# Fused joins, gate logits from joined rows, and scatters spread over three steps in a four-layer transformer kernel

## The chip, the core and the metric

The kernel runs on one core of a Trainium2 chip. The metric is the device time of one execution in microseconds (us). Matrix products run on TensorE (PE in the profile; its weight loads are PEld), element-wise work on VectorE (DVE), ScalarE (ACT) and GpSimd (POOL), and SyncE (SP) issues most of the transfers. The engines run in parallel, each takes its own instructions in program order, and they wait for each other by semaphores. Indirect transfers (scatters and gathers by index) are issued by GpSimd.

## What is computed

Two transformer layers on x of shape 4 x 512 x 256, each of an attention part and a feed-forward part. Every part takes normalised rows and is joined by another normalisation:

```python
x = x + _layernorm(_L0_attn_ref(_layernorm(x), ...))   # rms norm, rope, 16 heads, causal, + bo + residual
x = x + _layernorm(_L0_ffn_ref(_layernorm(x), ...))    # 8 experts, top 2, capacity 640 rows each
x = x + _layernorm(_L1_attn_ref(_layernorm(x), ...))   # causal attention
x = x + _layernorm(_L1_ffn_ref(_layernorm(x), ...))    # 8 small experts and a shared one, dense
```

The residual inside the first attention is its own input, the normalised rows. The first feed-forward sends rows to experts:

```python
probs = jax.nn.softmax(xr @ Wg, axis=-1)
gate_vals, expert_idx = jax.lax.top_k(probs, K)
pos = jnp.sum((jnp.cumsum(oh, axis=0) - 1) * oh, axis=1)      # rank of a row in its expert
kept = pos < C
dispatched = xr[dispatch_mask.reshape(-1) % S].reshape(E, C, d)
```

## The kernel before

The 2048 rows of x lie in SBUF as 16 tiles of 128 rows (`x`), with a second buffer of the same size (`sub`) for normalised rows and for the outputs of a part. The program is a chain of phases with a barrier of all engines between two: set-up, attention 0, experts, attention 1, dense.

**An attention phase** (`attention_phase`) walks 16 steps T, four head groups (g = T mod 4) for each of four batches (b = T div 4), and two steps behind them for what lags. A step has eleven slots s. In slot s TensorE fills a score bank whose row maxima VectorE takes (`unit_max`), and a second bank, three slots behind, that ScalarE turns into exponentials. GpSimd zeroes the upper triangle of these (`causal`, L494) at slots 0, 2 and 7. P·V of step T-2 stands at slots 2 and 5 of step T and waits for the selects. All other matrix work shares two banks in turn (`ps_m`): transposes, projections, P·V transposes ("otr"), output transposes ("ot"), output projections ("out"), and for the routing "rt" (transposes of the rows), "lg" (gate logits) and "rk" (ranks). `misc_plan` writes by hand in which step and slot each is filled and emptied. A filling waits until the last but one on its bank is empty. All engines walk the same slots in order, so one late engine holds the others back.

**Layer 0's extras.** GpSimd makes the residual (L513 and L516: normalised rows plus output bias), and VectorE adds it to the output projection's result (L1111), takes statistics, gets 1/sigma from GpSimd (`root`, a power), normalises `sub` tile by tile (L1135), adds it to x (L1141), and takes the new statistics. Only with the new mean and 1/sigma do `route_rows` (L1153) make normalised rows, which are transposed, multiplied by the gate weights, and go through `choose_top`, `choose_at`, `count`, `place` to a slot in the experts' buffer. `scatter` (L554) sends each tile by two indirect transfers. Batch 0's tiles are scattered in step 14, batch 1's in step 17, batches 2 and 3 behind the loop. The first expert's weights w1 are loaded at step 11, and split into a high and a low part in one piece each at step 13 (ScalarE L809, GpSimd L624).

**The passage to the experts.** The phase ends when all scatters have landed. After the barrier, `expert_phase` loads the first expert's rows (L1652), transposes them, and starts its matmuls.

**Attention 1** first gathers the experts' outputs (L562), weights and joins them (`combine_sum`, `combine_normalise`, `combine_add`), two batches ahead of its loop and two in it. **The dense phase** is one stream of matmuls; its last batch is joined behind the last of them by the class `Joining`.

## Time and profile before

| | us |
|---|---|
| median of 3 runs | 1114.74 |
| lowest and highest | 1113.88, 1115.35 |
| the profiled execution | 1114.21 |
| its span, first to last instruction | 1111.8 |

| engine | busy us | share of the span |
|---|---|---|
| TensorE | 943.1 | 85% |
| VectorE | 611.4 | 55% |
| ScalarE | 473.8 | 43% |
| GpSimd | 455.5 | 41% |

A busy share is an average over stages with different limits. The page's slices show TensorE below half of its time around 300 to 345 us (the passage to the experts) and again near 580 to 605 us (the passage to attention 1). Its clock is granted at two levels, full (1.00 in the rows) and half (0.50); a value between is an average over a stretch. Matmuls are pipelined, so that the durations of successive ones overlap: what one more costs is the distance of two starts. A row of a timeline gives start, duration, engine, line, operation, output and inputs, the count of merged instructions, and in brackets how long the engine had idled and for whom.

### The profile page before, as it was taken

How to read it: one execution, taken by the hardware profiler on the slowest of the kernel's cores; microseconds unless marked ns; L12 is line 12 of the kernel's file. 1: busy time of each engine (PE TensorE's matmuls, PEld its weight loads, DVE VectorE, ACT ScalarE, POOL GpSimd, SP SyncE). 2: the span in 40 equal slices, each digit the busy share in tenths (PEclk: the TensorE clock that was granted, in tenths of full speed). 3: DMA queues.
4: the chain of work that ended last, by engine and by line, in shares of the span. 5: the costliest groups of instructions: out<-in, count | busy, mean ns of one | idle time of the engine just before them, and what ended most of it. 6: DMA issues, size and time to landing. Idle time of an engine off the chain costs nothing. (4 is left out here: it accounts for less than half of the span.)

```text
span 1111.8 us, 17858 instructions
## 1 busy us (share of the span) xinstructions
PE 943.1 (85%) x6122; PEld 760.3 (68%) x6122; DVE 611.4 (55%) x1970; ACT 473.8 (43%) x838; POOL 455.5 (41%) x429
## 2 busy tenths in 40 slices
PE   3799999868418999999982779899999779999996
PEld 1467767645318999999981446566667558888885
DVE  7577787956613343333435766776666334553534
ACT  2156555634103343333336245556556433343331
POOL 3354653555441333222336523445243534634232
PEclk9799999978757999999995889999999979999998
DMA  4443213210123323333103752532410010000001
GB/s 138 170 158 101 86 30 124 68 52 1 48 73 141 116 99 117 123 123 123 61 27 110 219 183 81 164 98 91 161 59 29 1 48 1 1 20 1 20 1 38
DMA packets 50312, 91.78 MB, mean 83 GB/s; under 512 B 7360, under 2 KB 23104, under 8 KB 50112
## 3 DMA queue, kind: packets, MB, share of 16 engines
q1 hardware_dynamic: 47168, 82.49, 22.3%
q0 software_dynamic: 3072, 8.39, 2.4%
q8 instruction: 38, 0.62, 0.2%
q14 instruction: 34, 0.28, 0.1%
HBM read 54.55 MB, written 36.31 MB: 82 GB/s over the span
## 5 line engine op out<-in xcount | busy, mean ns | idle before, releaser
L795 ACT ACTIVATE a_probs<-a_ps_b 128x512 f32<-128x512 f32 x320 | 187.4, 602 | 171.1 <-PE a_ps_b L859 168.7
L1063 DVE CUSTOM_DVE_ANT_0 a_masked_s<-a_ps_a,a_mask_f 128x512 f32<-128x512 f32 (+1 forms) x256 | 154.4, 621 | 116.0 <-PE a_ps_a L843 110.7
L843 PE MATMUL a_ps_a<-a_k_st,a_q_st 128*128 128x256 f32 (+3 forms) x512 | 191.3, 421 | 15.7 <-DMA a_k_st<-scratch 12.5
L494 POOL TENSOR_SCALAR_AFFINE_SELECT a_probs<-a_probs 128x512 f32<-128x512 f32 x128 | 79.6, 639 | 182.7 <-ACT a_probs L795 182.3
L1711 POOL TENSOR_TENSOR w_lo<-w_raw,w_hi 128x2048 fp32r<-128x2048 f32 x16 | 74.0, 4627 | 174.1 <-ACT w_hi L1728 174.1
L859 PE MATMUL a_ps_b<-a_q_less,a_k_st 128*128 128x384 f32 (+3 forms) x512 | 133.0, 323 | 6.6 <-ACT a_probs L795 5.5
L843 PEld LDWEIGHTS a_ps_a<-a_k_st,a_q_st 128*128 128x128 f32 x512 | 96.0, 199 | 55.7 <-issue 34.2
L859 PEld LDWEIGHTS a_ps_b<-a_q_less,a_k_st 128*128 128x128 f32 x512 | 89.2, 191 | 30.1 <-ACT a_probs L795 22.0
L883 PE MATMUL a_ps_pv<-a_probs,a_v 128*32 128x512 f32 (+3 forms) x1024 | 90.4, 476 | 8.8 <-POOL a_probs L494 8.8
L1926 POOL TENSOR_TENSOR dense_h_lo<-dense_mixed,dense_h_hi 128x512 fp32r<-128x512 f32 x40 | 52.2, 1306 | 102.5 <-ACT dense_h_hi L1983 102.5
L1776 DVE SCALAR_TENSOR_TENSOR exp_h_lo<-exp_ps_u,exp_h_hi 128x320 fp32r<-128x320 f32 x128 | 61.4, 490 | 59.0 <-ACT exp_h_hi L1737 58.2
L1822 PE MATMUL exp_ps_o<-w_hi,exp_h_hi 128*128 128x256 f32 x320 | 92.5, 289 | 0.0
L1737 ACT ACTIVATE exp_h_hi<-exp_ps_u 128x320 fp32r<-128x320 f32 x128 | 54.2, 438 | 89.6 <-PE exp_ps_u L1804 89.6
L1822 PE MATMUL exp_ps_o<-w_hi,exp_h_lo 128*128 128x256 f32 x320 | 90.4, 283 | 0.0
L1822 PE MATMUL exp_ps_o<-w_lo,exp_h_hi 128*128 128x256 f32 x320 | 90.4, 283 | 0.0
L1804 PE MATMUL exp_ps_u<-exp_x_t_hi,w_hi 128*128 128x320 f32 x256 | 80.4, 314 | 1.1 <-DVE exp_x_t_lo L1756 1.1
L1804 PE MATMUL exp_ps_u<-exp_x_t_lo,w_hi 128*128 128x320 f32 x256 | 80.2, 313 | 0.0
L1804 PE MATMUL exp_ps_u<-exp_x_t_hi,w_lo 128*128 128x320 f32 x256 | 80.2, 313 | 0.0
L883 PEld LDWEIGHTS a_ps_pv<-a_probs,a_v 128*32 128x32 f32 x1024 | 28.2, 116 | 66.7 <-issue 55.2
L2164 DVE TENSOR_TENSOR dense_product<-dense_gated,dense_ps_u 128x512 f32<-128x512 f32 x40 | 27.5, 687 | 78.5 <-PE dense_ps_u L2000 72.8
L1822 PEld LDWEIGHTS exp_ps_o<-w_lo,exp_h_hi 128*128 128x128 f32 x320 | 61.3, 191 | 0.0
L1822 PEld LDWEIGHTS exp_ps_o<-w_hi,exp_h_lo 128*128 128x128 f32 x320 | 61.3, 191 | 0.0
(267 smaller groups left out, 2217.6 us busy)
## 6 DMA issues: line engine op xcount, KB each, us to landing
w_raw<-in_m_w SPq DMA_DIRECT2D x16, 1024.0 KB, 5.7
scratch<-a_hi SPq DMA_DIRECT2D x24, 512.0 KB, 2.8
scratch<-a_lo SPq DMA_DIRECT2D x24, 256.0 KB, 3.4
a_q_st<-scratch SPq DMA_DIRECT2D x64, 96.0 KB, 2.6
a_k_st<-scratch SPq DMA_DIRECT2D x64, 96.0 KB, 2.6
exp_rows<-dispatched SPq DMA_DIRECT2D x9, 640.0 KB, 3.9
dispatched<-kept_sub SPq DMA_DIRECT2D x9, 512.0 KB, 2.9
results<-exp_out SPq DMA_DIRECT2D x7, 640.0 KB, 4.0
```

Of the source, the lines that this page charges most:

```text
L494: nc.gpsimd.affine_select(out=blocks, in_=blocks, compare_op=ALU.is_ge, fill=0.0, base=0, pattern=[[0, HPG], [1, P]], channel_multiplier=- ...
L795: nc.scalar.activation(probs[:, k, :], ps_b[k % B_BANKS][:, :], ACT.Exp, scale=scale).then_inc(exps, 1)
L843: last = nc.tensor.matmul(ps[:, at:at + wd], q_st[t % STACKS][:, h // PER_TILE, i * P:wd], k_st[t % STACKS][:, h, 0:wd], start=True, stop= ...
L859: last = nc.tensor.matmul(ps[:, at:at + wd], k_st[t % STACKS][:, h, j * P:(j + 1) * P], q_less[:, h // PER_TILE, j * P:SEQ], start=True, s ...
L883: last = nc.tensor.matmul(ps_pv[h * VW:(h + 1) * VW, at:SEQ], v[:, b % 2, j, g * HPG + h, :], rhs, start=(j == 0), stop=(j == 2), skip_gro ...
L1063: nc.vector.tensor_tensor_reduce(masked_s[n % 2][:, 0:wd], ps[:, 0:wd], mask_f[:, SEQ - wd:SEQ], -1.0, -NEG, ALU.add, ALU.min, nmax[:, t % ...
L1711: nc.gpsimd.tensor_tensor(of["lo"][:, :, :], of["raw"][:, :, :], of["hi"][:, :, :].bitcast(F32), ALU.subtract).then_inc(ready, 1)
L1737: nc.scalar.activation(h[0][:, f, half * HALF:(half + 1) * HALF], ps_u[n % U_BANKS][:, 0:HALF], ACT.Relu).then_inc(u_hi, 1)
L1776: nc.vector.scalar_tensor_tensor(h[1][:, f, cols], ps_u[n % U_BANKS][:, 0:HALF], 0.0, h[0][:, f, cols].bitcast(F32), ALU.max, ALU.subtract ...
L1804: last = nc.tensor.matmul(ps_u[(2 * f + half) % U_BANKS][:, 0:HALF], (w1["hi"], w1["lo"])[i][:, c, f * P:(f + 1) * P], x_t[j][:, c * CAP + ...
L1822: last = nc.tensor.matmul(bank[:, t % 2 * D:(t % 2 + 1) * D], h[i][:, f, t * P:(t + 1) * P], (w2["hi"], w2["lo"])[j][:, f, :], start=(f == ...
L1926: nc.gpsimd.tensor_tensor(h[1][:, (m - 1) % H_BUFS, :], mixed[(m - 1) % 2][:, :], h[0][:, (m - 1) % H_BUFS, :].bitcast(F32), ALU.subtract) ...
```

## The change

In layer 0 and at the experts' join, x gets `sub * inv` without the mean taken off, in one instruction a tile. What is left over is the same number in every column of a row; it drops out of each later normalisation, and is kept in `shift` and subtracted in the dense phase's last join. The gate weights are centred (each column's mean taken off, "gc"), so that logits can come from the joined rows; ScalarE's exponential scales them by 1/sigma. The output bias goes into the projection as a matmul of a high and a low part, and VectorE adds x times 1/sigma to the result; GpSimd's residual is gone. The w1 load is issued in step 9, its split runs in quarters in steps 10 to 12. Scatters are two tiles a step in steps 14, 15 and 16; tiles 6 to 11 follow behind the loop, before and between the last two roots, and tiles 12 to 15 at the end. Choices and counts of batch 1 move from step 16 to step 14, those of batch 2 from step 17 to 16, the third batch's join to step 15, its output projection to slots 5 to 8 of step 14. The first expert's rows are loaded within attention 0, as soon as the scatters have landed.

```diff
@@ misc_plan
+        if rope and b == BATCH - 2:
+            put(("ot", b, 0), T + 2, 2, T + 2, 4)
+            put(("ot", b, 1), T + 2, 3, T + 2, 5)
+            put(("out", b, 0), T + 2, 5, T + 2, 7)
+            put(("out", b, 1), T + 2, 7, T + 2, 9)
...
+        early(("gc", 0, 0), 3)
...
-        put(("rt", 1, 0), 13, 9, 13, 10)
-        put(("rt", 1, 1), 13, 10, 14, 0)
+        early(("rt", 1, 0), 13)
+        middle(("rt", 1, 1), 13)
+        late(("lg", 1, 0), 13)
         put(("rk", 0, 0), 14, 0, 14, 2)
-        middle(("lg", 1, 0), 15)
-        put(("rk", 1, 0), 16, 8, 16, 9)
-        put(("rt", 2, 0), 17, 6, 17, 8)
-        put(("rt", 2, 1), 17, 7, 17, 9)
-        put(("lg", 2, 0), 17, 9, 17, 10)
-        final += [("rk", 2, 0), ("rt", last, 0), ("rt", last, 1), ("lg", last, 0), ("rk", last, 0)]
+        put(("rk", 1, 0), 15, 0, 15, 2)
+        put(("rt", 2, 0), 16, 0, 16, 2)
+        put(("rt", 2, 1), 16, 1, 16, 3)
+        put(("lg", 2, 0), 16, 3, 16, 5)
+        put(("rk", 2, 0), 17, 0, 17, 2)
+        final += [("rt", last, 0), ("rt", last, 1), ("lg", last, 0), ("rk", last, 0)]
@@ sync
-                if rope and T == 11:
+                if rope and T == 9:
                     sp.dma_start(w1["raw"][:, :, :], ...).then_inc(first_in, 16)
...
                 sp.wait_ge(second_in, 16)
+                sp.wait_ge(scattered, 16 * 2 * TILES)
+                sp.dma_start(w1["rows"][:, :, :], w["dispatched"][0:CAP, :]...).then_inc(keep["first_rows"], 16)
@@ gpsimd
-            def residual(b, i):
...
-                    if rope and T == 13 and s == 9:
-                        pool.wait_ge(first_hi, 1)
-                        nc.gpsimd.tensor_tensor(w1["lo"][:, :, :], w1["raw"][:, :, :], w1["hi"]..., ALU.subtract)
-                    if rope and T == 14 and s in (3, 5, 7, 9):
-                        scatter((s - 3) // 2)
-                    if rope and T == 17 and s in (3, 5, 7, 9):
-                        scatter(TPB + (s - 3) // 2)
+                    if rope and (T, s) in ((11, 3), (11, 4), (12, 3), (12, 5)):
+                        first_lower(2 * (T - 11) + s // (T - 7))
+                    if rope and T in (14, 15, 16) and s in (3, 8):
+                        scatter(2 * (T - 14) + s // 8)
...
             if rope:
+                for n in range(6, 11):
+                    scatter(n)
                 root(0, BATCH - 1)
+                scatter(11)
                 root(1, BATCH - 1)
-                for n in range(2 * TPB, TILES):
+                for n in range(12, TILES):
                     scatter(n)
@@ scalar
-                nc.scalar.activation(expd[:, b * TPB:(b + 1) * TPB, :], ex_in[...], ACT.Exp)
+                act.wait_ge(x_root, b + 1)
+                for n in range(b * TPB, (b + 1) * TPB):
+                    nc.scalar.activation(expd[:, n, :], ex_in[:, n, :], ACT.Exp, scale=rstd[:, n:n + 1])
@@ tensor
-                        pe.wait_ge(ry_ready, (b + 1) * TPB)
+                        pe.wait_ge(joined, b * TPB + 1)
...
+                        if kind == "rt":
+                            pe.wait_ge(joined, b * TPB + i + 1)
...
+                    biased = kind == "out" and rope
+                    if biased:
+                        pe.wait_ge(bias_split, 2)
+                        nc.tensor.matmul(ps[:, half * D:(half + 1) * D], spread_row[0:2 * VW, :], bias_rows[:, :], start=True,
+                                         stop=False)
@@ vector
-                dve.wait_ge(resid_ready, n + 2)
-                nc.vector.tensor_tensor(sub[:, n:n + 2, :], bank(name)..., resid[:, 2 * half:2 * half + 2, :], ALU.add)
+                for i in range(2):
+                    last = nc.vector.scalar_tensor_tensor(tile(sub, n + i), tile(x, n + i), rstd[:, n + i:n + i + 1],
+                                                          bank(name)[:, i * D:(i + 1) * D], ALU.mult, ALU.add)
...
+            def ln_join(b, i):
...
+                nc.vector.scalar_tensor_tensor(tile(x, n), tile(sub, n), inv[:, i:i + 1], tile(x, n), ALU.mult,
+                                               ALU.add).then_inc(joined, 1)
+                if i == TPB - 1:
+                    nc.vector.tensor_tensor(shift[:, b * TPB:(b + 1) * TPB], moments[:, 0, :, 0], inv[:, :], ALU.mult)
@@ place
-                after(nc.vector.tensor_scalar(fits[:, :, at], rank[:, :, at], float(CAP), None, ALU.is_lt))
-                after(nc.vector.tensor_scalar(far[:, :, at], fits[:, :, at], -2.0 * SLOTS, 2.0 * SLOTS, ALU.mult, ALU.add))
-                after(nc.vector.tensor_tensor(far[:, :, at], far[:, :, at], slot[:, :, at], ALU.add))
-                after(nc.vector.tensor_copy(put_at[:, :, at], far[:, :, at]))
-                dve.sem_inc(slots_ready, 1)
+                after(nc.vector.tensor_scalar(far[:, :, at], rank[:, :, at], float(CAP), 2.0 * SLOTS, ALU.is_ge, ALU.mult))
+                nc.vector.tensor_tensor(put_at[:, :, at], far[:, :, at], slot[:, :, at], ALU.add).then_inc(slots_ready, 1)
                 after(nc.vector.tensor_scalar(fits[:, :, at], rank[:, :, at], float(CAP), None, ALU.is_lt))
@@ vector, the steps
+                    from_s = 0 if rope and T == 15 else 6
...
+                    if rope and T == 15 and s in (6, 7, 8, 9):
+                        ln_join(2, s - 6)
                     if rope and T == 16 and s == 0:
-                        choose_at(1)
-                        count(1)
...
-                    if rope and T == 17 and s == 0:
+                    if rope and T == 16 and s == 8:
                         for i in range(TPB):
                             route_rows(2, i)
-                    if rope and (T, s) in ((13, 4), (17, 10)):
+                    if rope and (T, s) in ((13, 4), (14, 4), (16, 6)):
                         choose_at(min(T - 13, 2))
...
-                    if rope and (T, s) in ((14, 4), (16, 9)):
-                        weigh((T - 13) // 3)
+                    if rope and (T, s) in ((14, 6), (15, 5)):
+                        weigh(T - 14)
@@ expert_phase
-            load_rows(sp, 0, 0)
-            sp.wait_ge(rows_in[0], 16)
+            sp.wait_ge(keep["first_rows"], 16)
...
-            pe.wait_ge(rows_in[0], 16)
+            pe.wait_ge(keep["first_rows"], 16)
@@ Joining, before the dense phase's last normalisation
+            self.nc.vector.tensor_tensor(self.offset[:, :], self.moments[:, 0, :, 0], self.inv[:, :],
+                                         ALU.mult).then_inc(self.norm_chain, 1)
+            dve.wait_ge(self.norm_chain, k * self.CHAIN + 3)
+            self.nc.vector.tensor_tensor(self.offset[:, :], self.offset[:, :], self.shift[:, n0:n0 + TPB],
+                                         ALU.add).then_inc(self.norm_chain, 1)
```

The experts' join in attention 1 (`combine_join`) changes as `ln_join` does; its statistics move three slots forward.

## Rows read from the trace of the kernel before

**Rows 1.** Windows by step: 12, 13, 14, 15, then 16 to last P·V.

```profile
core 0: us, PE busy (x) PEld busy (x) DVE busy (x) ACT busy (x) POOL busy (x), PEclk, DMA share, GB/s
194.96:207.86 12.90, 12.90 (x106) 9.91 (x104) 12.02 (x45) 8.14 (x16) 4.13 (x7) 1.00 0.41 113
207.86:226.38 18.52, 10.55 (x79) 7.00 (x79) 17.03 (x58) 8.52 (x14) 11.85 (x10) 0.91 0.09 23
226.38:241.22 14.84, 14.75 (x95) 10.34 (x94) 10.08 (x46) 8.17 (x15) 6.47 (x7) 0.77 0.20 63
241.22:265.41 24.19, 16.20 (x110) 11.55 (x108) 11.61 (x46) 8.12 (x14) 16.85 (x19) 0.86 0.06 22
265.41:281.00 15.59, 11.93 (x91) 5.61 (x91) 13.18 (x56) 6.72 (x13) 7.56 (x11) 0.89 0.01 2
```

**Rows 2.** Timeline of step 13, GpSimd, VectorE and TensorE.

```profile
217.56 4.53 POOL L624 TENSOR_TENSOR w_lo<-w_raw,w_hi 128x2048 fp32r<-128x2048 f32 x1 [1.77 <-ACT w_hi L809]
217.82 4.90 DVE L1192 TENSOR_TENSOR a_hot<-a_numbers,a_top_atf 128x32 f32<-128x32 f32 x2
225.81 1.11 PE L931 MATMUL a_ps_m<-kept_ident,kept_sub 128*128 128x128 f32 x4 [5.85 <-DVE kept_sub L1100]
```

**Rows 3.** Step 15's timeline; groups of residuals and scatters (ns min/median/max; landing).

```profile
249.03 1.82 POOL L494 TENSOR_SCALAR_AFFINE_SELECT a_probs<-a_probs 128x512 f32<-128x512 f32 x3
250.31 1.93 PE L883 MATMUL a_ps_pv<-a_probs,a_v 128*32 128x512 f32 x8 [6.29 <-POOL a_probs L494]
...
L513 POOL TENSOR_SCALAR a_resid<-kept_x,kept_mean,kept_rstd 128x256 f32<-128x256 f32 x16 | 19.6, 1226 | 0.1
...
L554 POOL DMA_INDIRECT dispatched<-kept_sub,a_put_at x32: 968/973/1242, 234.2 to 325.2; - x32
...
DMA to landing us min/median/max: 2.4/2.4/3.3
```

**Rows 4.** Timeline of step 17, GpSimd and TensorE.

```profile
277.34 1.82 POOL L494 TENSOR_SCALAR_AFFINE_SELECT a_probs<-a_probs 128x512 f32<-128x512 f32 x3 [1.21 <-ACT a_probs L795]
...
283.14 0.63 PE L892 MATMUL a_ps_m<-kept_ident,a_pv_sb 128*128 128x128 f32 x4 [0.33 <-ACT a_ry_t L716]
285.40 1.09 PE L931 MATMUL a_ps_m<-kept_ident,kept_sub 128*128 128x128 f32 x8
```

**Rows 5.** Timeline from the last batch's output to the experts.

```profile
295.08 1.04 POOL L521 TENSOR_TENSOR a_inv<-a_var_eps,kept_minus_half 128x4 f32<-128x4 f32 x1 [5.26 <-DVE a_var_eps L1128]
296.55 1.38 DVE L1135 TENSOR_SCALAR kept_sub<-kept_sub,a_moments,a_inv 128x256 f32<-128x256 f32 x4
304.19 1.94 PE L931 MATMUL a_ps_m<-kept_ident,kept_sub 128*128 128x128 f32 x8 [11.29 <-DVE kept_sub L1153]
306.90 3.55 PE L911 MATMUL a_ps_m<-early_g,a_ry_t 128*128 128x8 f32 x16 [0.77 <-ACT a_ry_t L716]
310.49 0.19 DVE L1168 COPY a_logits<-a_ps_m 128x32 f32<-128x32 f32 x1 [6.44 <-PE a_ps_m L911]
313.94 0.28 DVE L1205 TENSOR_TENSOR a_picked<-a_hot,a_ps_m 128x32 f32<-128x32 f32 x2 [0.45 <-PE a_ps_m L920]
316.29 0.97 POOL L554 DMA_INDIRECT dispatched<-kept_sub,a_put_at  x1 [3.73 <-DVEq L1217]
...
325.24 0.97 POOL L554 DMA_INDIRECT dispatched<-kept_sub,a_put_at  x1 [0.30 <-issue]
331.80 0.37 SPq L1652 DMA_DIRECT2D exp_rows<-dispatched  x1
335.81 1.97 PE L1794 MATMUL exp_ps_t<-kept_ident,exp_rows 128*128 128x128 f32 x8 [21.90 <-DMA exp_rows<-dispatched]
```

**Rows 6.** A fused operation, the experts' add, and reduced-precision matmuls (chain: start, us).

```profile
L1265 DVE SCALAR_TENSOR_TENSOR kept_sub<-a_rows,gates 128x256 f32<-128x256 f32 x16 | 7.7, 484 | 0.6
...
599.43 1.23 DVE L1291 TENSOR_TENSOR kept_x<-kept_x,kept_sub 128x1024 f32<-128x1024 f32 x1
...
928.56 1.41 PE dense_ps_d L2000 x12
```

More of the change, by code:

```diff
@@ L580, in _ @@
                 route_tables()
-                pool.wait_ge(keep["early_in"]["bias_o"], 16)
             else:
@@ L914, in fill @@
                         last.then_inc(full, 1)
+                elif kind == "gc":
+                    pe.wait_ge(gate_ones, 1)
+                    for c in range(KC):
+                        last = nc.tensor.matmul(ps[:, 0:E0], ones_f[:, :], w_g[:, c, :], start=(c == 0), stop=(c == KC - 1))
+                    last.then_inc(full, 1)
                 elif kind == "rk":
```

199 lines of the change are left out of this document (101 added, 98 removed).

## Prediction

> **What bounds the kernel now.** I read the view of windows by step first. In the first attention layer TensorE sets the pace up to step 12: it is busy for 12.90 of that step's 12.90 us, VectorE for 12.02 (93%) [rows 1]. Then it stops doing so. Step 13 takes 18.52 us with 10.55 of TensorE, step 15 takes 24.19 with 16.20, part of it at a lower clock (0.86 granted on average) [rows 1]. So the loss lies in waits, and the timelines name them.
>
> In step 13 TensorE idles 5.85 us for VectorE's attention rows. VectorE had two tiny comparisons (128x32) in flight for 4.90 us, which start 0.26 us after GpSimd's 4.53 us subtraction of w1 and end just behind it [rows 2]. In step 15 TensorE idles 6.29 us, then starts P·V as the causal selects arrive: GpSimd did them only at 249.03, since four tiles' scatters and two residual tiles stood ahead in its queue [rows 3]. A scatter instruction takes 0.97 us and its successor starts 1.28 us later; a tile has two, so 2.55 us. A residual tile starts with a 1.23 us instruction, 16 of them are 19.6 us [rows 3], and an add follows each.
>
> The third place is the passage to the experts, a serial chain: output projection of the last batch, join, statistics, normalised rows, transposes, gate logits, choice, ranks, then eight scatters on GpSimd, then the load of expert 0's rows [rows 4, 5]. TensorE idles there for 11.29 us, then for 21.90 us [rows 5].
>
> **The change, part by part.** The sum is made against the profiled execution: 1114.21 us, span 1111.8; the rest is 2.4 us. The median of the runs is 1114.74, 0.5 above it.
>
> *Bias on TensorE.* Each half of an output projection gets two 128x256 matmuls of a reduced-precision kind. Nearest row: twelve such in 1.41 us, 0.12 each [rows 6]; the other bound is the full-precision gate matmul at a low clock, 16 in 3.55 us, 0.22 each [rows 5]. Batches 0 and 1 lie in steps where TensorE is the bound: 8 x 0.15 = 1.2, plus the two gate-centring matmuls, 0.3. **+1.5** (1.0 to 2.1). The cover for those of batch 2 is counted in step 14.
>
> *Residuals leave GpSimd.* The 19.6 us and the adds leave GpSimd; VectorE pays two instructions of 0.48 us, some 0.9, for one of 0.7 per half (the 0.48 is from the same operation on other tiles [rows 6]; the 0.7 is half the 128x1024 add's 1.23, rounded up [rows 6]). In steps bound by TensorE neither counts; what they free is in the next terms.
>
> *Step 13.* The w1 split moves to steps 10 to 12 in quarters; a quarter of 4.53 is 1.1 us [rows 2]. With the pair of comparisons back at 0.3, VectorE's 17.03 falls to 12.4; at step 12's 93% that is 13.4 us. I take 14.0 instead of 18.52: **-4.5** (-5.0 to -3.5). A quarter can still hold a two-input join of step 12 for 1.1 us, beneath TensorE's 12.90.
>
> *Step 14* gets more. VectorE had 10.08 us [rows 1]; it gains choice, indices and counts of tile group 1 (the same chain takes 3.45 us in the tail, of which TensorE and hand-overs are 0.5, so 3.0 [rows 5]) and two output evacuations, 1.8: 14.9, or 16.0 at 93%. TensorE gains three of four output halves, four bias matmuls and half a logits fill, about 3.1 + 0.6 + 0.9, and loses what the half clock cost it in this step (0.77 granted): 14.75 x 0.77 = 11.4, plus 4.6 = 16.0. Both at 16, and the output now starts right behind ScalarE's evacuation (about 1.2 us of exposure): 17.3. **+2.5** (+1 to +6).
>
> *Step 15.* GpSimd has two tiles' scatters (5.1 us) instead of a backlog, no residuals. VectorE had 11.61 [rows 1]; less one choice (0.6) and two evacuations (1.4), plus ranks (1.1), gates (1.3), four fused joins (1.8): 13.8, or 14.9 at 93%. I take 15.5 against 24.19: **-8.7** (-10.5 to -5).
>
> *Steps 16 and 17* up to the last P·V, 15.59 us [rows 1]: joins and counts of group 1 leave VectorE's front and the selects come sooner, a gain of about 2; transposes and logits of group 2 come in with two waits on ScalarE's copies, a loss of about 2. **0** (-2 to +3).
>
> *The tail.* The last head-group's transposes no longer wait behind group 2's route copies (283.14, released by them, could start near 281.7), and the output transposes need not stand behind sixteen gate matmuls (285.40, could start at 283.1) [rows 4]: -2.3. Bias and evacuations +1.0; GpSimd's root starts at 293.9 instead of 295.08. GpSimd must by then be through tiles 6 to 10, ten scatter instructions from 279.2, the end of the last selects [rows 4]: 12.8 us, free at 292.0, with 1.9 us to spare. Joins begin at 295.05 (before: 296.55, held by the ranks of group 2 [rows 5]). Here lies the core: the transposes start behind the first join, at 295.5, instead of behind add, statistics, root and rows at 304.19 [rows 5]. Two copies and the 3.55 us of logits follow; the choice starts at 302.5 (before 310.49), place at 305.9 (313.94), and with one conversion and two small operations less the scatters start at 307.6 instead of 316.29 [rows 5]. The statistics, root and rows now run beside the logits and end at 301.6. **-8.7** (-10 to -5).
>
> *Row load inside the phase.* From the last scatter's issue (325.24) to SP's load is 6.6 us, to TensorE's first transpose 10.6 [rows 5]. A scatter lands in 2.4 us [rows 3]; then the load (4.0) now runs beside the phase's end instead of behind it. Hidden is the lesser of the load's 4.0 and the phase change's 331.80 - 327.9 = 3.9: **-3.7** (-3.9 to -2).
>
> *Second layer and dense part.* A join of four normalisations and one add (1.38 + 1.23) becomes four fused at 0.48 or less, overlapped as the normalisations are, about 1.5 [rows 5, 6]. Once on the head's path: -1.1; twice in steps where VectorE is busiest: -1.5 together (0 to -2.4). The dense tail gets two dependent operations of 128x4 before its last normalisation; a 128x32 copy is 0.19 [rows 5]: +0.4. The rest of this is beside matmuls. **-2.2**.
>
> Sum: 1.5 - 4.5 + 2.5 - 8.7 + 0 - 8.7 - 3.7 - 2.2 = -23.8. **Predicted 1090.4 us.**
>
> **Weighed against the Trainium skill.** Row: the 4.90 us comparison has two inputs in SBUF and lies beside a GpSimd read of SBUF [rows 2]. "SBUF — State Buffer", Who interferes with whom, says that such a pair shares a lock which the loser waits out. It speaks against the fused join: it has two SBUF inputs too, where the normalisation that it replaces has one. By that rule each of steps 12 and 15 could lose up to a 1.1 us quarter or a 0.6 us select [rows 4]. Without the rule those terms are zero; both fit into the bounds above.
>
> **The rivals.**
> *A, scatters slow beside VectorE (8%).* The scatter row's longest is 1.24 us against 0.97 [rows 3], in the step where VectorE worked beside it. If tiles 6 to 10 now all meet a busy VectorE, ten are 0.27 longer; 2.7 less 1.9 of slack delays the root by 0.8, and those during the loop delay selects by about 1 a step: 1090.4 + 0.8 + 3 = 1094. The same page's section on its two sides has a descriptor writer locked out while VectorE runs a two-port operation, which is this mechanism. The tail's scatters at a steady 0.97 beside an idle VectorE [rows 5] neither confirm nor refute it.
> *B, the steps give nothing back (20%).* Steps 13 to 15 lose 57.55 - 46.8 = 10.7 by my count. But choices, counts and output projections are packed into step 14, and every misc fill alternates over two banks. If it takes 21 and step 16 loses 4, what remains is 3: 1114.2 - 23.8 + 7.7 = 1098. Against it: the 5.85 and 6.29 us gaps have one named cause each, and both causes go.
> *C, no gap, no half clock (10%).* If TensorE never drops to half clock in steps 13 to 15, step 14 gains another 2, step 15 reaches 14, and the tail's output matmuls gain 3: 1083.
> *D, slower (4%).* TensorE stays at half clock. After the 5.85 us gap the granted clock averages 0.77 over step 14 [rows 1]. Steps 13 to 16 hold 53.4 us of TensorE work, some 47 at full clock. If waits of 1 to 2 us, scattered by the two banks, keep it at half, they need 94 where the four steps now take 73: +21, less tail, load and second layer (14.7), plus 1.5 for the bias: +8, 1122. It decides once more than two thirds of that work runs at half clock. Against it: step 12 runs at 1.00 with TensorE never free.
> *E, the load doesn't help (8%).* If the phase's end waits for the transfer in flight, the 3.7 stay: 1094.
>
> **How the numbers follow.** Forecast 50%, A 8, B 20, C 10, E 8, D 4. The range reaches C and B with the spread of the step terms: 1081 to 1102. What can be told from no change is about 0.2%, 2.2 us: faster 0.95, same 0.02, slower 0.03.
>
> **What would show it.** The comparisons in step 13 at 0.3 us; no TensorE wait above 2 us for GpSimd's selects; step 14 near 17 and step 15 near 15; route transposes released by a join and not by rows; scatters of tile 12 some 27 us after the last P·V of the layer ends (281), now 35; expert transposes 8 us after the last scatter's issue, now 10.6; a join of the second layer 1.1 us shorter. I am wrong if GpSimd's backlog reaches the root of the last batch, or if step 14 passes 21 us.

## The result and the profile after

The changed kernel takes 1109.5 us (median of 20 executions), the kernel before beside it on the same chip 1113.8: a ratio of 0.9964, 95% interval 0.9951 to 0.9978. Two later measurements of the same pair gave 0.9974 (0.9954 to 0.9993) and 0.9972 (0.9955 to 0.9989). So it is faster, by 3 to 4 us; 24 were forecast, and the range ended at 1102.

The profiled execution took 1110.99 us with a span of 1109.3, so the two traces compared below stand 2.5 us apart in their spans. First the windows by step, for the steps of [rows 1] and in the same columns:

```profile
199.24:211.96 12.72, 12.72 (x106) 9.91 (x104) 12.43 (x44) 8.14 (x16) 7.52 (x10) 1.00 0.40 115
211.96:226.43 14.47, 13.70 (x103) 9.53 (x102) 11.38 (x56) 8.33 (x18) 2.96 (x5) 0.88 0.11 29
226.43:249.75 23.32, 18.36 (x110) 12.18 (x110) 14.60 (x71) 9.07 (x19) 6.44 (x8) 0.93 0.13 40
249.75:264.66 14.91, 10.99 (x79) 6.86 (x79) 14.39 (x59) 6.23 (x12) 7.87 (x10) 0.99 0.10 35
264.66:288.66 24.00, 20.29 (x112) 11.94 (x111) 8.72 (x49) 8.34 (x15) 10.54 (x13) 0.58 0.09 32
```

Steps 13 and 15 are as short as forecast. Step 14 is 8.5 us longer than before and the last stretch, to the last P·V, 8.4 us longer, with TensorE at a granted 0.58. Step 12 ends at 211.96 against 207.86 [rows 1]: 4.1 us had been lost by then.

VectorE's comparisons of step 13, which had been held for 4.90 us [rows 2], are short again (the timeline of VectorE):

```profile
222.84 0.29 DVE L1226 TENSOR_TENSOR a_hot<-a_numbers,a_top_atf 128x32 f32<-128x32 f32 x2
```

TensorE's timeline of step 14 has three new waits, named in the brackets:

```profile
228.28 0.63 PE L895 MATMUL a_ps_m<-a_identr,a_nm 128*128 128x128 f32 x4 [1.30 <-DVE a_logits L1202]
230.51 1.12 PE L962 MATMUL a_ps_m<-kept_ident,kept_sub 128*128 128x128 f32 x4 [1.08 <-DVE a_picked L1239]
238.53 0.35 PE L982 MATMUL a_ps_m<-a_bias_rows,a_spread_row 64*128 64x256 f32 x1 [2.15 <-ACT a_o_t L715]
```

The first two wait for a misc bank that VectorE still reads (group 1's logits, group 0's ranks), the third for ScalarE's copy of batch 2's transposed rows, right ahead of the projection that now follows it. Of the last stretch TensorE's timeline shows:

```profile
264.00 0.33 PE L962 MATMUL a_ps_m<-kept_ident,kept_x 128*128 128x128 f32 x1 [1.64 <-DVE kept_x L1174]
265.21 1.09 PE L895 MATMUL a_ps_m<-a_identr,a_nm 128*128 128x128 f32 x4 [0.53 <-DVE a_nm L1125]
267.99 1.12 PE L962 MATMUL a_ps_m<-kept_ident,kept_x 128*128 128x128 f32 x4 [1.16 <-ACT a_ry_t L732]
273.67 1.03 PE L935 MATMUL a_ps_m<-a_w_gc,a_ry_t 128*128 128x8 f32 x8 [1.25 <-ACT a_ry_t L732]
275.13 1.71 PE L935 MATMUL a_ps_m<-a_w_gc,a_ry_t 128*128 128x8 f32 x8
284.49 4.17 PE L906 MATMUL a_ps_pv<-a_probs,a_v 128*32 128x512 f32 x32 [0.34 <-POOL a_probs L520]
```

The rows of L962 and L935 are group 2's route transposes and gate logits, all but the last behind a wait. The last P·V takes 4.17 us here, and took 2.36 before:

```profile
278.62 2.36 PE L883 MATMUL a_ps_pv<-a_probs,a_v 128*32 128x512 f32 x32 [0.80 <-POOL a_probs L494]
```

The tail, from the timelines of all engines:

```profile
303.61 1.04 POOL L537 TENSOR_TENSOR a_inv<-a_var_eps,kept_minus_half 128x4 f32<-128x4 f32 x1 [5.48 <-DVE a_var_eps L1166]
305.31 2.42 PE L962 MATMUL a_ps_m<-kept_ident,kept_x 128*128 128x128 f32 x8 [4.11 <-DVE kept_x L1174]
308.50 3.55 PE L935 MATMUL a_ps_m<-a_w_gc,a_ry_t 128*128 128x8 f32 x16 [0.77 <-ACT a_ry_t L732]
315.55 0.28 DVE L1239 TENSOR_TENSOR a_picked<-a_hot,a_ps_m 128x32 f32<-128x32 f32 x2 [0.46 <-PE a_ps_m L949]
317.45 1.04 POOL L579 DMA_INDIRECT dispatched<-kept_sub,a_put_at  x1 [7.89 <-DVE a_put_at L1248]
326.46 0.97 POOL L579 DMA_INDIRECT dispatched<-kept_sub,a_put_at  x1 [0.30 <-issue]
328.94 0.36 SPq L499 DMA_DIRECT2D exp_rows<-dispatched  x1
333.11 1.30 PE L1822 MATMUL exp_ps_t<-kept_ident,exp_rows 128*128 128x128 f32 x5 [17.60 <-DVEq L1778]
```

From root to route transposes it is 1.7 us, before 9.1 [rows 5]; from the last scatter's issue to the experts' transposes 6.65, before 10.57 [rows 5].

### The profile page after: what moved, and what is told of

It reads as the page before. It is cut to its first block and busy times, and to the rows that moved or that the text cites. A ratio compares the mean times of both kernels' runs of the same rounds, so it can differ in the third digit from the quotient of the medians.

```text
span 1109.3 us, 17911 instructions
## 1 busy us (share of the span) xinstructions
PE 960.0 (87%) x6142; PEld 766.7 (69%) x6142; DVE 601.8 (54%) x1986; ACT 477.1 (43%) x855; POOL 425.9 (38%) x402
## 3 DMA queue, kind: packets, MB, share of 16 engines
q1 hardware_dynamic: 47168, 82.49, 22.1%
## 5 line engine op out<-in xcount | busy, mean ns | idle before, releaser
L866 PE MATMUL a_ps_a<-a_k_st,a_q_st 128*128 128x256 f32 (+3 forms) x512 | 191.2, 421 | 14.8 <-DMA a_k_st<-scratch 12.4
L906 PE MATMUL a_ps_pv<-a_probs,a_v 128*32 128x512 f32 (+3 forms) x1024 | 93.8, 491 | 1.1 <-POOL a_probs L520 1.1
```

The source lines that it names most:

```text
L866: last = nc.tensor.matmul(ps[:, at:at + wd], q_st[t % STACKS][:, h // PER_TILE, i * P:wd], k_st[t % STACKS][:, h, 0:wd], start=True, stop= ...
L906: last = nc.tensor.matmul(ps_pv[h * VW:(h + 1) * VW, at:SEQ], v[:, b % 2, j, g * HPG + h, :], rhs, start=(j == 0), stop=(j == 2), skip_gro ...
```

## The experiments

Ratios are to the kernel before, run beside each kernel on the same chip, with a 95% interval. In some groups of runs the kernel before had a median of 1114 to 1115 us, in others of 1122 to 1123 (one chip showed both), so times are compared within a group and ratios across them. Ratios across the two kinds of group agree only to some 0.4%: one kernel ran in both (`warm` and `warm_again`) and came at 0.9830 and 0.9871. The changed kernel itself ran in groups at 1114 to 1115 only. Lengths of steps come from one profile each. The windows in the fences have the columns of [rows 1].

**1. The form of the bias matmul** (`bias_wide`).

```diff
-bias_rows, spread_row = sb("bias_rows", [2 * VW, D], F32R), ...   # 64 rows, weights 1/32
+bias_rows, spread_row = sb("bias_rows", [P, D], F32R), ...        # 128 rows, weights 1/64
-nc.tensor.matmul(ps[...], spread_row[0:2 * VW, :], bias_rows[:, :], start=True, stop=False)
+nc.tensor.matmul(ps[...], spread_row[:, :], bias_rows[:, :], start=True, stop=False)
```

> The changed kernel with the bias matmul over 128 rows instead of 64 (rows of weight 1/64 instead of 1/32). Theory 1 (the price lies in the 64-row form): in steps 7 and 11 each half of an output projection takes 1.09 us from its start to the next group's start with the bias and 0.67 to 0.72 without, so 0.40 per bias matmul; if the 64-row weight load between 128-row ones is what can't run ahead, a 128-row one costs about 0.15, steps 7 and 11 fall from 17.49 to about 16.4 each, the tail's output by about 1, and the whole by about 3 us. Theory 2 (a matmul of this kind costs 0.4 with any number of rows): steps 7 and 11 stay at 17.4 to 17.5 and the time stays within 0.5 us.

Ratio 0.9901 (0.9880 to 0.9921). Steps 7 and 11 took 15.98 us each instead of 17.49 (15.51 in the kernel before), so 1.5 us for four matmuls. One row tile of a projection (four to a batch; the expectation calls it a half) in TensorE's timeline, the kernel before (without bias), the changed one, and the 128-row form; each ends where the next group starts:

```profile
124.97 1.03 PE L948 MATMUL a_ps_m<-early_o,a_o_t 128*128 128x256 f32 x4
125.64 0.58 PE L843 MATMUL a_ps_a<-a_k_st,a_q_st 128*128 128x512 f32 x1
```

```profile
124.25 0.38 PE L982 MATMUL a_ps_m<-a_bias_rows,a_spread_row 64*128 64x256 f32 x1
124.56 1.13 PE L985 MATMUL a_ps_m<-early_o,a_o_t 128*128 128x256 f32 x4
125.34 0.59 PE L866 MATMUL a_ps_a<-a_k_st,a_q_st 128*128 128x512 f32 x1
```

```profile
124.34 0.33 PE L982 MATMUL a_ps_m<-a_bias_rows,a_spread_row 128*128 128x256 f32 x1
124.50 1.03 PE L985 MATMUL a_ps_m<-early_o,a_o_t 128*128 128x256 f32 x4
125.18 0.58 PE L866 MATMUL a_ps_a<-a_k_st,a_q_st 128*128 128x512 f32 x1
```

That is 0.67, 1.09 and 0.84 us. By these rows a 64-row matmul among 128-row ones costs 0.4 (0.5 by the steps, 17.49 against 15.51), a 128-row one 0.12 to 0.17: theory 1. The weight loads show where: the load for the next group starts 0.31 us behind the 64-row bias matmul (124.25 and 124.56), and 0.05 us behind the 128-row one (124.34 and 124.39). The gain was not free of the clock: step 14, with the same instructions and shorter ones for the bias, took 25.04 us at a granted 0.80 here, 23.32 at 0.93 in the changed kernel.

**2. Group 2's fills back at the end** (`rt2_late`).

```diff
-put(("rt", 2, 0), 16, 0, 16, 2)
-put(("rt", 2, 1), 16, 1, 16, 3)
-put(("lg", 2, 0), 16, 3, 16, 5)
-put(("rk", 2, 0), 17, 0, 17, 2)
+put(("rt", 2, 0), 17, 6, 17, 8)
+put(("rt", 2, 1), 17, 7, 17, 9)
+put(("lg", 2, 0), 17, 9, 17, 10)
...
```

The ranks now follow the last output projection. VectorE's choice, counts and places of group 2 move with them, and the scatters of tiles 8 to 11, so only tile 8 is left between the last two roots.

> The changed kernel with group 2's route transposes, logits, choice, counts and ranks back at the end of step 17 and behind it, where the kernel before has them; joins, statistics and rows of group 2 stay where the change put them. Theory 1 (these fills, put between the score units of step 16, with waits of 1.2 us on ScalarE's copies, stretch the step and leave TensorE at half clock behind them): steps 16 and 17 up to the last P.V take 15 to 17 us instead of 24.0, granted clock there above 0.8; about 2.3 us come back between the last P.V and the output transposes and 1.1 for the ranks ahead of the joins; net 3 to 5 us faster than the changed kernel, 1104 to 1107. Theory 2 (the stretch comes from the joins and statistics on VectorE and the scatters on GpSimd, which stay): 21 us or more, and the kernel is 1 to 3 us slower than the changed one.

Ratio 0.9895 (0.9877 to 0.9913). Its windows: the stretch to the last P·V, then from there to the end of the last output projection.

```profile
266.19:281.95 15.76, 12.81 (x90) 6.17 (x91) 4.37 (x18) 6.52 (x12) 8.33 (x11) 0.83 0.11 38
281.95:302.88 20.93, 17.20 (x59) 12.47 (x58) 4.99 (x29) 3.90 (x9) 2.55 (x3) 0.59 0.07 24
```

The stretch lost 8.2 us although joins, statistics and the loop's scatters stayed: theory 2 falls. The run does not separate TensorE's fills from the choice and counts that moved with them; but VectorE was busy for only 8.72 of the stretch's 24.00 us, and TensorE's waits there name ScalarE's copies. The passage behind it took 20.9 us (12.6 in the changed kernel's first profile), so I took the gain for given back. The median and experiment 8 show that it is not.

**3. Batch 2's output projection later** (`out2_shift`).

```diff
-put(("out", b, 0), T + 2, 5, T + 2, 7)
-put(("out", b, 1), T + 2, 7, T + 2, 9)
+put(("out", b, 0), T + 2, 7, T + 2, 9)
+put(("out", b, 1), T + 2, 9, T + 3, 0)
```

> The changed kernel with batch 2's output projection two units later in step 14 (halves at units 7 to 10 instead of 5 to 8). Theory 1 (step 14 is 23.3 us long because of TensorE's waits of 1.3, 1.1 and 2.15 us and the half clock behind them; the third is the output right behind ScalarE's copy): the third wait goes, step 14 falls to about 21, step 15 grows by at most 1, net 1 to 2 us faster. Theory 2 (step 14 is bound by VectorE's added choice and counts, TensorE's waits only show it): the wait moves elsewhere, step 14 stays above 22.5 and the time within 0.5 us.

Ratio 0.9940 (0.9919 to 0.9961). Step 14 took 23.78 us and step 15 18.46; the granted clock fell to 0.72 and 0.90. Neither theory had step 15's 3.5 us more: with the clock in play, this run does not tell the two apart.

**4. Added work on TensorE** (`filler`, then `warm`). A filler is a matmul whose result is overwritten, in a bank that is free, ahead of an instruction that waits.

```diff
+def fillers(ps, count):
+    for _ in range(count):
+        nc.tensor.matmul(ps[:, 0:2 * P], w_qk[:, 0, 0, :], w_qk[:, 0, 0:2, :], start=True, stop=True)
+fillers(ps_pv, {(14, 1): 2, (14, 2): 2, (15, 1): 3, (16, 0): 3, (16, 1): 3}.get((T, s), 0))
+fillers(ps, {("out", 2, 0): 4, ("lg", 2, 0): 2, ("otr", 15, 0): 2, ("ot", 3, 0): 2,
+             ("out", 3, 0): 2, ("rt", 3, 0): 8, ("lg", 3, 0): 1}.get(name, 0))
```

(`filler` has 512 columns and the counts of its expectation.)

> The changed kernel with 23 extra 128x512 matmuls on TensorE whose results are thrown away, put ahead of its waits: 3 and 2 at units 1 and 2 of step 14, 5 ahead of batch 2's output projection, 3 at unit 1 of step 15, 4 and 3 at units 0 and 1 of step 16 and 3 ahead of group 2's logits; about 0.45 us each at full clock, 10 us in all against 10.3 us of waits. Theory 1 (the loss in steps 14 and 16 to 17 is TensorE's half clock after stretches of waits): the granted clock from the end of step 15 to the last P.V rises from 0.58 to above 0.8, this stretch falls from 24.0 to 18 to 21 us in spite of the added work, and the time falls by 2 to 5 us. Theory 2 (the loss is the order of the work and the waits themselves, the clock only a companion): the stretch stays at 24 or more and the time rises by 0 to 5 us.

Ratio 0.9949 (0.9928 to 0.9970), no gain that can be told from the changed kernel's 0.9964 to 0.9974. But a filler took 0.91 us, not 0.45 (five in 4.56), so 21 us were put into 10 us of waits. The windows of step 14 and of the stretch:

```profile
223.57:250.12 26.55, 25.69 (x132) 15.83 (x133) 14.59 (x71) 9.07 (x19) 6.44 (x8) 1.00 0.11 36
265.53:289.34 23.81, 20.63 (x131) 11.14 (x129) 9.63 (x49) 8.20 (x15) 10.83 (x13) 0.93 0.10 34
```

The clock did come up, and the stretch carried some 6 us of fillers in the same time (0.8, 2.74 and 2.74 us of three groups; the first ran mostly ahead of it). Half the size then, with the changed kernel itself beside it:

`after_again`, the changed kernel:

> The changed kernel itself, as the measure for the others of this group on the same chip. Both theories expect a ratio to the kernel before of 0.995 to 0.998 and steps as in its first profile: 23.3 us for step 14, 14.9 for step 15, 24.0 from there to the last P.V.

`warm`:

> The changed kernel with extra 128x256 matmuls on TensorE whose results are thrown away, fewer and smaller than before: where the first filler kernel's took 0.91 us each (4.56 us for five) I expect 0.45 now; 4 at units 1 and 2 of step 14, 4 ahead of batch 2's output, 3 at unit 1 of step 15, 6 at units 0 and 1 of step 16, 2 ahead of group 2's logits, then 2, 2 and 2 ahead of the last transposes and output projection, 8 ahead of the last route transposes and 1 ahead of the last logits. Theory 1 (half clock is what stretches this part; fillers that fit into the waits are free): step 14 falls to 21 to 22 us, the stretch to the last P.V to 18 to 20, an output half of the last batch from 2.07 us to 1.1 and its logits from 3.55 to 1.9; in all 8 to 12 us faster than the changed kernel. Theory 2 (order and waits, clock only a companion): the times of these stretches stay within 1 us, apart from the single matmuls' own lengths, and the whole within 2 us.

The changed kernel came at 0.9974, `warm` at 0.9830 (0.9809 to 0.9851): 1112.7 and 1097.4 us, 15 us less with more work. The windows of the last stretch and of the passage from there to the end of the last output projection, first of the changed kernel, then of `warm`, there with step 14 ahead of them:

```profile
265.15:289.20 24.05, 20.31 (x111) 11.89 (x111) 8.68 (x49) 8.35 (x15) 10.61 (x13) 0.58 0.09 33
289.20:303.98 14.78, 12.08 (x32) 7.25 (x32) 2.31 (x6) 2.73 (x7) 7.32 (x8) 0.60 0.22 75
```

```profile
225.74:249.29 23.55, 22.47 (x129) 16.54 (x130) 14.63 (x72) 9.09 (x19) 6.45 (x8) 0.93 0.13 40
264.21:283.66 19.45, 16.88 (x122) 10.95 (x120) 9.07 (x49) 8.18 (x15) 9.26 (x12) 0.82 0.08 29
283.66:294.16 10.50, 10.05 (x46) 7.08 (x46) 2.31 (x6) 2.61 (x7) 8.06 (x9) 1.00 0.30 105
```

Theory 1 holds for the stretch and the passage; it fails for step 14, which stayed at 23.55.

**5. With the 128-row bias too** (`warm_wide`: experiment 1's edit and `warm`'s).

> The same with the bias matmul over 128 rows too. Its price fell from 0.38 to 0.12 us each in steps 7 and 11 (17.49 to 15.98 each); the two are independent, so a further 3 us off in the two steps and 0.6 to 1 in the last output projection: 3.5 us less than the kernel with the small fillers alone. Rival: less work on TensorE means a lower clock again and nothing is left of it behind step 13.

Ratio 0.9816 (0.9798 to 0.9835), 3.0 us below `warm` in the same group: the two add up.

**6. Group 1's logits, choice and counts in step 15** (`lg1_later`).

```diff
-late(("lg", 1, 0), 13)
-put(("rk", 1, 0), 15, 0, 15, 2)
+middle(("lg", 1, 0), 15)
+put(("rk", 1, 0), 16, 0, 16, 2)
+choose_at(1) at (15, 9), count(1) at (15, 10), weigh(1) at (16, 5)
```

> The changed kernel with group 1's logits, choice and counts in units 6 to 10 of step 15 instead of the end of step 13 and units 4 to 8 of step 14, its ranks at the head of step 16. Theory 1a (step 14's excess over my 17.3 comes from TensorE's wait for the bank that the logits' reader frees, 1.3 us, from VectorE's 3.0 us of choice and counts and the half clock behind): step 14 falls from 23.3 to 19 or 20, step 15 rises by 2 to 3, net within 1.5 us. Theory 1b (step 14's excess is the output projection of batch 2 that went there, TensorE work of 16.6 us at full clock, and the wait of 2.15 us for ScalarE's copies): step 14 stays above 22, step 15 rises by 2 to 3.

Ratio 0.9950 (0.9931 to 0.9970). Step 14 fell by 1.3 us to 22.0, about the wait for the logits' bank; step 15 rose by 3.7 to 18.65, more than either theory had, at a granted 0.82 instead of 0.99. That is nearer 1b: the choices are 1.3 us of what makes step 14 long.

**7. Fillers elsewhere, and in the kernel before** (`before_warm`, `best`, `warm_wide_out2`, `warm_again`, `warm_mid`, `warm_tail`, `eq_before`).

`before_warm`:

> The kernel BEFORE with extra 128x256 matmuls whose results are thrown away (0.45 us each at full clock) in TensorE's long waits: 12 at the end of step 13, 13 ahead of P.V in step 15, 4 and 2 in step 16, 1 in step 17, then 1, 2 and 2 ahead of the last transposes and output, 22 ahead of the last route transposes, 1 ahead of the last logits. Theory 1 (clock after waits): step 14 falls from 14.84 to 12 or 13 us (its granted clock was 0.77), the start of step 16 gains 1, the last output projection falls from 5.4 us to about 3 and the last transposes and logits from 5.5 to 3; 6 to 9 us faster than before. If so the change with its own fillers (15 us faster than it is without) is worth more at equal clock than the 4 us that were measured: 1100 or so against 1107. Theory 2 (fillers act otherwise than by the clock): no gain here, 0 to 2 us slower.

Ratio 0.9922 (0.9899 to 0.9944), 8.4 us faster. Steps 14, 15 and the stretch, at full clock throughout:

```profile
227.16:241.36 14.20, 13.34 (x101) 9.54 (x99) 10.14 (x46) 8.16 (x15) 7.35 (x8) 1.00 0.24 75
241.36:262.88 21.52, 20.30 (x135) 16.36 (x135) 11.49 (x46) 7.91 (x14) 16.02 (x19) 1.00 0.06 19
262.88:277.08 14.20, 12.28 (x99) 6.32 (x98) 13.07 (x56) 6.72 (x13) 7.58 (x11) 1.00 0.00 1
```

So the kernel before was losing to the clock as well.

`best`:

> The changed kernel with the 128-row bias and the small fillers, and more of them: 27 behind the last ranks of the first layer, while the scatters run; 4 at the head of the expert phase; 10 ahead of the second layer's first transposes, released by the first join. Theory 1: the first expert's 27 matmuls at a 0.27 us pitch go to 0.145 (3 us), the second layer's first projections from 6.3 us to 4.2 (2 us) and its transposes from 1.94 to 1.1: another 3 to 5 us off 1094.4 (on a chip where before takes 1115.5), ratio 0.977 to 0.979. Rival: TensorE's idle time in the change of phase (some 4 us) is enough for the clock to fall again, and only the second layer's 2 to 3 us come.

Ratio 0.9831 (0.9806 to 0.9857), no better than `warm_wide`, which ran in a group of the other kind. The second layer's first projections did fall from 6.3 to 3.67 us; the first expert's matmuls still started at half clock (0.27 us from start to start), behind a wait of 4.11 us: the rival. Whether its 2 to 3 us are in the whole can't be told across the groups.

`warm_wide_out2`:

> The changed kernel with the 128-row bias, the small fillers and batch 2's output projection two units later (halves at units 7 to 10 of step 14), without the four fillers ahead of it. At half clock this move gave step 14 nothing (23.8, clock 0.72) and cost step 15 3.5 us (clock 0.90). Theory 1 (that was the clock; the wait of 2.15 us for ScalarE's copies is real and goes): step 14 falls from 22.2 to 20 or 21, step 15 rises from 14.3 to 15 or 16, the whole within 1 us. Theory 2 (VectorE, which has 14.6 us of work in the step, or ScalarE decides): step 14 stays at 22 and step 15 rises by more than 1.5.

Ratio 0.9838 (0.9817 to 0.9860). Step 14 took 20.06 us and step 15 16.18, in all 36.24; `best` (this projection earlier, four fillers ahead of it, and 41 more from behind the ranks on) 22.14 and 14.33, in all 36.47. The whole took 1106.3 us, `best` 1104.6. What was moved came with its waits: close to theory 1.

`warm_again`:

> The changed kernel with all the small fillers, once more, as the measure on this chip for the three beside it. Theory 1 expects a ratio to the kernel before of 0.981 to 0.986 as on the first chip. If it is above 0.99 here, its first 15 us were in part that chip's.

`warm_mid`:

> Only the 19 fillers of steps 14 to 16. Theory 1: the stretch from step 15 to the last P.V falls from 24.0 to 19 or 20, the last output projection stays at half clock (7 to 10 us from its start to its end against 5.5 with fillers); 5 to 8 us faster than the changed kernel alone, ratio 0.989 to 0.992. Theory 2 (the stretch's loss is made good later anyway): no faster than 0.995.

`warm_tail`:

> Only the 15 fillers behind the last P.V. Theory 1: steps 14 to 17 as in the changed kernel (23.3, 14.9, 24.0), the last output projection, transposes and logits at full clock or near it; 4 to 7 us faster, ratio 0.990 to 0.993. Theory 2 (the two parts only work together, since two fillers cannot lift the clock out of a long stretch at half): within 2 us of the changed kernel.

`eq_before`:

> The kernel before with fillers, more of them in the three long waits than in the first such kernel (19, 21 and 36 instead of 12, 13 and 22), since one takes 0.27 us and not 0.45. Theory 1: 8 to 10 us faster than before, ratio 0.991 to 0.993; beside the changed kernel with fillers on the same chip this gives what the change is worth where neither loses to the clock: 8 to 12 us. Rival: the whole gain of the change is the same with and without fillers, 3 to 5 us, and this kernel comes out at 0.987 or below.

`warm_again` 0.9871 (0.9848 to 0.9895), `warm_mid` 0.9888 (0.9868 to 0.9907), `warm_tail` 0.9925 (0.9904 to 0.9946). Against the changed kernel's 0.9964 to 0.9974, from groups of the other kind, the fillers of steps 14 to 16 work alone; those behind the last P·V seem to, by little more than such ratios differ. `warm_again`'s windows of step 14, step 15 and the stretch, all at full clock:

```profile
226.86:249.42 22.56, 21.12 (x132) 15.18 (x130) 14.58 (x71) 9.09 (x19) 6.45 (x8) 1.00 0.14 42
249.42:264.35 14.93, 13.16 (x92) 8.63 (x91) 14.41 (x59) 6.29 (x13) 7.90 (x10) 1.00 0.10 36
264.35:282.65 18.30, 14.72 (x122) 9.24 (x120) 9.19 (x49) 8.14 (x15) 9.56 (x12) 1.00 0.10 33
```

`eq_before` came at 1.0005 (0.9987 to 1.0023). Its premise was my misreading: a filler is two matmuls in the records, so it takes 0.5 us and not 0.27, and 36 of them overran the wait for the last route rows: from the end of the last output projection to the last logits it took 20.08 us, 13.16 with 22 fillers. It says nothing on the change. The better measure is `before_warm` against `warm_again`, from two groups in which the kernel before took 1123.0 and 1121.9: 0.9871 / 0.9922 = 0.9949, 5.7 us. The two intervals together leave 2 to 9 us, and `warm`'s 0.9830 in its place would give 10. So it is not shown that the change is worth more than its 4 us where neither kernel loses much to the clock; 24 us it is not.

**8. Group 2's fills back, with the 128-row bias** (`warm_wide_rt2` with `warm`'s fillers and two more, `wide_rt2` without; the edits of experiments 1 and 2).

`warm_wide_rt2`:

> The changed kernel with the 128-row bias, the small fillers, and group 2's route transposes, logits, choice, counts and ranks back at the end of step 17 and behind it. At half clock that move took 8.2 us out of the stretch to the last P.V and put 8.4 in behind it. Theory 1 (both were the same TensorE work and waits, moved): at full clock the stretch takes 15 to 16 us instead of 19.3, the one behind it 12.5 to 14 instead of 8.9, the whole within 1.5 us of the kernel with the bias and the fillers alone. Theory 2 (early fills cost more than their work): 2 us faster or better.

Ratio 0.9781 (0.9755 to 0.9807), against 0.9831 for `best` in the same group, 5.2 us less, though `best` has some 40 fillers more. The stretch and the passage behind it, at full clock:

```profile
257.32:270.85 13.53, 10.67 (x91) 5.36 (x91) 4.63 (x18) 6.52 (x12) 9.06 (x12) 1.00 0.13 45
270.85:286.41 15.56, 12.90 (x78) 11.23 (x78) 4.99 (x29) 3.79 (x9) 2.54 (x3) 1.00 0.09 31
```

`best` had 18.31 and 17.77 there: 4.8 us gained in the stretch and nothing given back in this pair. Theory 2, by the medians. (The passage itself is no measure: it took 8.9 us in `warm_wide`, in a group of the other kind; see the last section.)

`after_third`, the changed kernel:

> The changed kernel itself, as the measure for the one beside it on this chip. Expected ratio to the kernel before 0.995 to 0.998, as twice before; on a chip where before takes 1122 us the passage from the last P.V to the end of the last output projection, 12.6 and 14.8 us in its two profiles, should be 16 to 20 as in all profiles of other kernels from such chips.

`wide_rt2`:

> The changed kernel with two of its steps mended and nothing else, no fillers: the bias matmul over 128 rows, and group 2's route transposes, logits, choice, counts and ranks back at the end of step 17 and behind it. Theory 1 (the bias is 3 us in steps 7 and 11 and up to 1.5 in the last output; the early fills of group 2 cost 4 to 5 us of waits and work and about 4 of half clock in the stretch to the last P.V, of which the passage behind it takes back 3 to 5): 5 to 8 us faster than the changed kernel, ratio to before 0.988 to 0.991. Theory 2 (what the stretch gains, the passage gives back whole at half clock): 3 to 4 us, ratio 0.991 to 0.995.

`after_third` 1111.1 us, `wide_rt2` 1097.1 us, ratio 0.9837 (0.9815 to 0.9858): 14 us faster than the changed kernel beside it and 17.5 faster than before, without any added work and beyond both theories. Its windows of steps 14 and 15, the stretch, and the passage:

```profile
223.31:249.27 25.96, 20.09 (x110) 13.29 (x110) 14.50 (x71) 9.04 (x19) 6.71 (x8) 0.80 0.11 36
249.27:265.18 15.91, 12.12 (x75) 6.84 (x75) 14.21 (x59) 6.82 (x13) 8.79 (x11) 0.86 0.10 34
265.18:281.08 15.90, 12.95 (x90) 6.23 (x91) 4.37 (x18) 6.51 (x12) 8.34 (x11) 0.82 0.10 37
281.08:293.70 12.62, 11.31 (x58) 9.64 (x58) 5.00 (x29) 3.77 (x9) 2.54 (x3) 0.73 0.11 39
```

The spans of the two profiles differ by 6.9 us only (1105.8 and 1098.9): 3.2 by the end of step 12, 8.1 in the stretch, less 3.7 in steps 14 and 15, where the granted clock is lower (0.80 and 0.86, against 0.93 and 0.99). The profiled execution of the one was its second fastest of 12, that of the other its slowest of 5; where the other half of the 14 us lies, these profiles can't say. This is the version to take of those without added work.

## Why the prediction was wrong

The forecast was 24 us and the measured gain 3 to 4. Term by term, forecast against the two profiles:

| term | forecast | measured |
|---|---|---|
| bias on TensorE, to the end of step 12 | +1.5 | +4.1 |
| step 13 | -4.5 | -4.1 |
| step 14 | +2.5 | +8.5 |
| step 15 | -8.7 | -9.3 |
| steps 16 and 17 to the last P·V | 0 | +8.4 |
| last P·V to the first scatter of tile 12 | -8.7 | -6.5 |
| row load in the phase | -3.7 | -3.9 |
| second layer and dense part | -2.2 | +0.2 |

Two more profiles of the changed kernel (`after_again`, `after_third`) give the terms down to the last P·V within 0.5 us of these. The tail is -4.3 in the one, where the last output projection is at half clock throughout, and -6.5 in the other, and the last term is -5.4 and -3.3: its +0.2 is one profile's, and -2.2 is not shown to be wrong.

What I had argued from named waits held: the comparisons, GpSimd's backlog, the route transposes behind the joins, the load beside the phase's end. Rivals A and E are out: root waits for the variance and not for scatters (303.61), and the load's 3.9 us came whole.

*Steps 16 and 17 (forecast 0) are the step that failed, in size and in kind.* I had "a loss of about 2" for group 2's transposes and logits against "a gain of about 2". At full clock with fillers the stretch takes 18.3 us with them and 13.5 without: the early fills cost 4.8, their own matmuls plus two waits on ScalarE's copies (1.16 and 1.25 us in the changed kernel), each in line ahead of the score units on which the last P·V depends. The other part is the half clock: 24.0 against 18.3, 5.7 us, where the kernel before lost 1.4 (15.6 against 14.2). So of the 8.4 us the runs with fillers put 4.1 to placement (18.3 against 14.2) and 4.3 to the clock. This is rival D's mechanism in part: TensorE falls to half behind waits of 1 to 2 us. I gave it 4% as an all-or-nothing case over four steps. It came in one stretch, and there TensorE stays at half for 13 us without another such wait; why is open.

*Step 14 (+2.5) failed on waits, not on work.* At full clock (`warm_again`) TensorE was busy for 21.1 us, 4.6 of them fillers: 16.5 of its own, against my 16.0. But I had counted one exposure of 1.2 us where the rows show 1.30, 1.08 and 2.15 and smaller ones. Clock is about 1 us here (23.3 against 22.1 to 22.6; `warm`, at 0.93, had 23.6). This is rival B, step 14 beyond 21 us, with its "every misc fill alternates over two banks".

*The bias (+1.5) was mis-sized.* I priced 128-row matmuls, at 0.15, and those do cost 0.12 to 0.17. The diff has 64 rows: 0.4 to 0.5 each. Steps 7 and 11 took 17.49 us each, before 15.51: 4.0 of the 4.1 us. The shape stood in the diff; the nearest row of the trace had another.

*The tail (-8.7)*: its serial part came as forecast. Of the missing 2.2 us, 2.0 are lost ahead of the root, most of them in the last output projection: 5.38 us before, 7.83 now, where I had put 1.0 for bias and evacuations. That is the 64-row bias again and not a lower clock, for the granted clock is the same in both, 0.68 (the row of the kernel before, its window, and the changed kernel's window):

```profile
287.48 5.38 PE L948 MATMUL a_ps_m<-early_o,a_o_t 128*128 128x256 f32 x16 [0.99 <-ACT a_o_t L699]
287.48:292.86 5.38, 5.38 (x18) 4.30 (x18) 2.40 (x10) 0.00 (x0) 1.96 (x2) 0.68 0.23 78
293.38:301.21 7.83, 7.82 (x20) 4.63 (x20) 1.63 (x4) 0.52 (x3) 3.83 (x4) 0.68 0.23 84
```

A row tile of it takes 2.5 us from start to start at half clock and 1.4 at full, with 128 rows 1.9 and 1.0 (`best`, `warm_wide`). Full clock would have saved both kernels time here.

*The second layer (-2.2)*: the head's join gave its 1.1 (TensorE's wait ahead of the first transposes is 24.1 to 24.3 us, before 25.2). Its first six steps took 103.85 us before, 103.5 to 103.6 in three profiles of the changed kernel: 0.3 for the forecast 1.5. The dense part (first transposes to the end of the span) took 219.8 us before and 220.9, 217.3 and 217.2 in three profiles of the changed kernel, so that single profiles can't settle the rest.

*Weighed rule.* I had set the Trainium skill's "SBUF — State Buffer", Who interferes with whom, against the fused join, at up to 1.1 us in each of two steps. The trace agrees for VectorE's instructions: of step 12's four joins, the three that lie beside GpSimd's selects and w1 quarters (199.68 to 204.36) took 0.96, 0.90 and 0.67 us, the fourth 0.48:

```profile
200.80 0.96 DVE L1174 SCALAR_TENSOR_TENSOR kept_x<-kept_sub,a_inv,kept_x 128x256 f32<-128x256 f32 x1
205.03 0.48 DVE L1174 SCALAR_TENSOR_TENSOR kept_x<-kept_sub,a_inv,kept_x 128x256 f32<-128x256 f32 x1
```

The step lost nothing by it (12.72 us, before 12.90), since TensorE is its bound, which the bounds of the forecast had covered. What bore on this case is a section that I had not weighed: the Trainium skill's "TensorE: Matmul & The Clock Gate", A second HAM failure mode, has TensorE's clock swing between its levels where groups of matmuls cycle through PSUM banks with short idle times between them. The trace agrees in this: the granted clock falls to half between 264 and 265 us, behind waits of 0.94 and 1.64 us that end at 259.63 and 264.00; it is back at 1.00 from 272 to 274, and falls again behind one of 1.25. From 275 to 288 it then stays at half, with no wait above 0.34 us. Not all of the waits are for a bank: of 1.64, 0.53 and 1.16 us the last is, for ScalarE's copy out of it, the other two are for data.

## What to carry to other kernels

Price a moved fill at full clock and at half, and count each wait in line ahead of it, not its matmuls alone: group 2's early fills are 3.9 us of matmuls in the rows above (1.12, 1.03 and 1.71, at half and full clock) and cost 8.2. Where TensorE is often short of work, put a few spare matmuls into its waits and read the granted clock: it tells in one run how much of a slow stretch is clock, provided that the fillers fit into the waits (8 of 0.5 us in a 4 us wait helped, 36 in an 11 us wait cost 7 against 22). Keep odd shapes out of a stream of full-height matmuls: here repeated rows made the bias matmul 0.25 to 0.4 us cheaper (zero-filled ones were not tried). And a stretch made shorter can leave the next one at a lower clock, as step 14 of `bias_wide` and `wide_rt2` shows (0.80 instead of 0.93).

## What the runs showed of the hardware that was not expected

Step 13 has the same instructions in all these kernels, and took 12.87 us at a granted 1.00, 14.47 at 0.88 and 15.88 at 0.79, in different profiles (`rt2_late`, the changed kernel, `warm_tail`), in each behind a wait of 0.42 or 0.43 us. The changed kernel's 20 executions spread from 1107.1 to 1119.7; that such steps are the reason is likely and not shown, since each has one profile.

```profile
212.32:225.19 12.87, 12.10 (x103) 9.22 (x102) 11.39 (x57) 8.34 (x18) 2.97 (x5) 1.00 0.13 32
```

In the groups of runs in which the kernel before took 1122 us or more, eleven of twelve profiles had 15 to 21 us between the last P·V and the end of the last output projection. In `best` and `warm_wide_out2` TensorE has waits of 1.5 to 2.5 us there, and ScalarE of 2.1 and 2.8, that no instruction of the trace explains. In the groups at 1114 to 1115, eight of eight had 8.9 to 14.8. The kernels differ in what stands in the passage, but `warm` and `warm_again` are one kernel and took 10.5 and 17.2 us. The cause stays open.
